# First stage of a fused attention and linear block laid out anew, and an order rule for the tiled matmuls

## The reference, cut to what matters

```python
def _layernorm(x): return (x - mean(x)) / sqrt(var(x) + 1e-5)

# x: (4, 2048, 512) float32; Wq, Wk, Wv, Wp: (512, 512); 16 heads of 32
h = _layernorm(x)
q, k, v = heads(h @ Wq + bq), heads(h @ Wk + bk), heads(h @ Wv + bv)
att = q @ k.T / sqrt(32)
att = where(tril and (column % 4 != 3), att, -inf)     # every fourth key is never seen
y = softmax(att) @ v
x = x + _layernorm(y @ Wp + bp)
# one of eight (512, 512) matrices is chosen by argmax(log_softmax(logits) - log(-log(u)))
x = x + _layernorm(_layernorm(x) @ W[idx] + b[idx])
```

## Time and profile before

| | us |
|---|---|
| median of 3 runs | 2775.3 |
| lowest, highest of them | 2772.9, 2775.33 |
| the profiled execution | 2770.63 |
| its span, first to last instruction | 2768.8 |
| TensorE busy | 2555.6 (92%) |
| VectorE busy | 1972.0 (71%) |
| ScalarE busy | 1615.7 (58%) |
| GpSimd busy | 1484.0 (54%) |

### The profile page before, as it was taken

The page is one execution under the profiler, slowest core; times in us unless marked ns, Lnnn a source line. Parts: engine busy times, 40 slices in busy tenths (PEclk is TensorE's granted clock), DMA queues, the critical chain, the costliest instruction groups (busy, mean ns, idle before and its releaser), DMA issues.

```text
span 2768.8 us, 46168 instructions
## 1 busy us (share of the span) xinstructions
PE 2555.6 (92%) x17416; PEld 1014.9 (37%) x17416; DVE 1972.0 (71%) x4199; ACT 1615.7 (58%) x2781; POOL 1484.0 (54%) x1350
## 2 busy tenths in 40 slices
PE   1999999999999999999999999999999999999985
PEld 0444333333343433333344433333334343333222
DVE  8667876876587687787566778678647767677623
ACT  4556656666655566566665555666665565655662
POOL 2335465665546366376653547467455635546563
PEclk7999999999999999999999999999999999999997
DMA  4211110010021111001011211101002110100000
GB/s 130 76 33 55 36 46 21 22 41 16 25 64 54 39 37 48 15 26 40 11 50 48 63 37 45 33 14 41 11 21 68 50 33 25 51 16 18 20 1 19
DMA packets 89192, 103.98 MB, mean 38 GB/s; under 512 B 11562, under 2 KB 61578, under 8 KB 88970
## 3 DMA queue, kind: packets, MB, share of 16 engines
q1 hardware_dynamic: 88970, 101.04, 12.3%
HBM read 39.59 MB, written 16.78 MB: 20 GB/s over the span
## 4 chain that ended last, share of the span: by engine, by line
PE 64%; DVE 22%; ACT 5%; POOL 4%; issue 3%; DMA 1%; SPq 1%; POOLq 0%; ACTq 0%; DVEq 0%
PE psO L1045 13%; PE psM L1004 11%; PE psS L1028 10%; DVE MP L807 9%; PE psU L1061 8%; PE psW L981 7%; PE psW L982 6%; PE psW L983 6%; ACT P L710 3%; DVE SC L826 2%; DVE STA L773 2%; DVE XR L785 2%; PE psS L1031 1%; DVE XP L793 1%; PE psM L1007 1%
## 5 line engine op out<-in xcount | busy, mean ns | idle before, releaser
L710 ACT ACTIVATE P<-psS,EX 128x512 f32<-128x512 f32 (+2 forms) x1920 | 1122.0, 631 | 668.3 <-PE psS L1028 357.4
L807 DVE TENSOR_REDUCE MP<-psM 128x1 f32<-128x512 f32 (+8 forms) x2112 | 1107.8, 560 | 502.1 <-PE psM L1004 269.0
L581 POOL TENSOR_TENSOR P<-P 128x512 f32<-128x512 f32 x576 | 725.5, 1288 | 119.6 <-ACT P L710 118.9
L1004 PE MATMUL psM<-KST,QST 96*128 96x512 f16 (+8 forms) x2112 | 640.0, 335 | 59.1 <-DVE MP L807 47.2
L1028 PE MATMUL psS<-QST,KST 98*128 98x512 f16 (+2 forms) x1920 | 618.9, 357 | 29.5 <-ACT P L710 22.3
L1045 PE MATMUL psO<-P,V 128*32 128x512 f32 (+2 forms) x3840 | 463.2, 554 | 10.6 <-ACT P L710 8.9
L586 POOL TENSOR_TENSOR SC<-SC 128x512 f32<-128x512 f32 x64 | 83.7, 1307 | 554.9 <-DVE SC L826 554.9
L1004 PEld LDWEIGHTS psM<-KST,QST 96*128 96x128 f16 x2112 | 200.8, 97 | 466.6 <-DVE MP L807 272.4
L1028 PEld LDWEIGHTS psS<-QST,KST 98*128 98x128 f16 x1920 | 171.1, 97 | 405.2 <-issue 190.0
L1061 PE MATMUL psU<-P,ONES 128*32 128x512 f32 (+2 forms) x2688 | 299.3, 517 | 0.0
L826 DVE RECIPROCAL SC<-SC 128x128 f32<-128x128 f32 x256 | 231.7, 929 | 79.5 <-ACT SC L718 79.5
(11 more groups left out here) (129 smaller groups left out, 3152.7 us busy)
## 6 DMA issues: line engine op xcount, KB each, us to landing
XB<-in_L_attn_x_dram SPq DMA_DIRECT2D x64, 256.0 KB, 2.7
XR<-in_L_attn_x_dram SPq DMA_DIRECT2D x64, 256.0 KB, 2.7
QST<-QKH SPq DMA_DIRECT2D x128, 128.0 KB, 3.2
out_dram<-XR SPq DMA_DIRECT2D x64, 256.0 KB, 2.0
KST<-QKH SPq DMA_DIRECT2D x128, 96.0 KB, 2.6
QST<-QKL SPq DMA_DIRECT2D x64, 128.0 KB, 3.3
KST<-QKL SPq DMA_DIRECT2D x64, 96.0 KB, 2.7
QST<-MROW SPq DMA_DIRECT2D x128, 4.0 KB
```

What stands on the lines that cost most here:

```text
L581: e.tensor_tensor(P[:, acc, a, :], P[:, acc, a, :], P[:, buf, a, :], ALU.add).then_inc(g_s, 1)
L710: e.activation(P[:, p_buf[u, g, sb_], a, t0:512], psS[:, s_slot[step] % 2, t0:512], ACT.Exp, scale=EX[:, 1:2]).then_inc(a_e, 1)
L807: e.tensor_reduce(MP[:, j, r, a, ci:ci + 1], psM[:, m_slot[s] % 2, 0:n], AX.X, ALU.max).then_inc(v_m, 1)
L1004: i = e.matmul(psM[:, k, 0:n], QST[0:96, h, 128 * r:128 * r + 128], KST[0:96, h, c0:c0 + n], start=True, stop=not last)
```

## The change

1. Loads on two queues. SyncE issues x, the two small rows, the identity, then the biases; ScalarE issues Wk, Wq, Wv, the mask and Wp (`load_w` is now a step of ScalarE). `choose` is cut in two on VectorE, and constants are written first.
2. Wider splits. `whigh` and `wlow` of Wq and Wk are 4 instructions of 128x512 each in place of 16 of 128x128.
3. `absmax` is cut into one step for each matrix (`wmax`), one for the biases (`bmax`) and the all-reduce (`allmax`, 1200 ns in the table). Wp, the chosen matrix and the fold get late ranks (0.1 to 0.5); the fold is cut in three, and projections wait for the split of their own weight alone. A pseudo engine `hbm` stands for the landing of the weights in the scheduler.
4. In the scheduler, when TensorE's last step was a `pv` or a `sum`, a ready `pv` or `sum` is taken before any other step.

```diff
-        add("sp", -99, 9000, ("load_w",), [("sp", "load_x", 0, 3)])
-        add("act", -99, 5500, ("choose",), [("sp", "load_w")])
-            add("gp", (-90, -65)[n], 3000, ("absmax", n), [("dve", "absmax", n)])
+        add("act", -100, 2600, ("load_w",))
+        for i, n in enumerate((1, 0, 2, 3)):
+            add("hbm", -100 + i, 2700, ("land", n), [("act", "load_w")])
+        for n, at in enumerate((-89, -90, -88, 0.1, 0.15)):
+            add("dve", at, 2250, ("wmax", n), [("hbm", "land", n), ("dve", "consts")])
+        for n, at in enumerate((-87, 0.2)):
+            add("gp", at, 1200, ("allmax", n), [("dve", "bmax"), ("dve", "scales", 0)][n:n + 1]
+                + [("dve", "wmax", i) for i in ((0, 1, 2), (3, 4))[n]])
...
+        for n, at in ((1, -60), (0, -59), (2, -58), (3, 0.3), (4, 0.4)):
+            add("act", at, 2400 if n < 2 else 2000, ("whigh", n), [("dve", "scales", int(n > 2))])
+            add("dve", at, 2400, ("wlow", n), [("act", "whigh", n)])
...
+        add("dve", 0.5, 3200, ("fold", 2), [("dve", "fold", 1), ("dve", "wlow", 3), ("dve", "wlow", 4)])
...
-                for at, (rank, key) in enumerate(ready[e]):
+                tiled = e == "pe" and self.pe and self.pe[-1][0] in ("pv", "sum")
+                for at, (rank, key) in sorted(enumerate(ready[e]),
+                                              key=lambda x: tiled and x[1][1][1] not in ("pv", "sum")):
...
+                if kind == "load_w":
+                    for n, w in ((1, Wk), (0, Wq), (2, Wv)):
+                        e.dma_start(stage[n], w.rearrange("(k p) n -> p k n", p=128)).then_inc(d_w[n], 16)
...
-                        for k in range(4):
-                            for m in range(4):
-                                c = slice(128 * m, 128 * m + 128)
-                                e.activation(WH[:, n, k, c].rearrange("p (d a) -> p a d", a=4),
-                                             stage[n][:, k, c].rearrange("p (a d) -> p a d", a=4), ACT.Copy,
-                                             scale=SW[:, n:n + 1]).then_inc(a_w, 1)
+                        for a in range(4):
+                            e.activation(heads_apart(WH, n, a), heads_in(stage[n], a), ACT.Copy,
+                                         scale=SW[:, n:n + 1]).then_inc(a_w, 1)
```

More of the change, by code:

```diff
@@ L68, in __init__ @@
             self.finish(u)
-        self.pe, self.act, self.dve, self.gp, self.sp = ([] for _ in range(5))
+        self.pe, self.act, self.dve, self.gp, self.sp, self.hbm = ([] for _ in range(6))
         self.run()
@@ L87, in startup @@
-        add("act", -98, 5400, ("kconst",), [("dve", "consts")])
[L88 to L93, removed]
@@ L178, in attend @@
                     was = self.P_WAS.get((u, g, sb))
-                    held = [("dve", "wlow", 2)]
+                    held = [("dve", "wlow", n) for n in range(3)]
                     if was:
@@ L423, in sandwich_block @@
         DV = counted(order.dve, lambda s: {
-            "choose": ("p", 6), "consts": ("c", 8), "absmax": ("p", 2 if s[-1] else 6),
-            "scales": ("p", 7 if s[-1] else 19), "wlow": ("w", 16 if s[-1] in (0, 1) else 1),
-            "fold": ("f", 18 if s[-1] else 1), "stats": ("ln", 4), "norm": ("n", 1), "cast": ("n", 1),
+            "choose": ("p", 4 if s[-1] else 2), "consts": ("c", 7), "ident": ("c", 1), "wmax": ("p", 1), "bmax": ("p", 3),
+            "scales": ("p", 7 if s[-1] else 19), "wlow": ("w", 4 if s[-1] in (0, 1) else 1),
+            "fold": ("f", 17 if s[-1] == 2 else 1), "stats": ("ln", 4), "norm": ("n", 1), "cast": ("n", 1),
             "high": ("q", 1), "peak": ("m", 1), "peaks": ("m", 3), "invert": ("o", 1)}[s[0]])
         GP = counted(order.gp, lambda s: {
-            "absmax": ("c", 1), "rstd": ("ln", 1), "low": ("p", 1), "rest": ("q", 1), "add": ("s", 1),
+            "allmax": ("c", 1), "rstd": ("ln", 1), "low": ("p", 1), "rest": ("q", 1), "add": ("s", 1),
             "scale": ("o", 1), "olow": ("o", 1), "add_x": ("r", 1), "add_y": ("r", 1)}[s[0]])
+        staged = max(DV["wlow", n] for n in range(3))
         w_job = [s[1] if s[0] == "proj" else s for s in order.pe
@@ L672, in _ @@
                     elif name == "v":
-                        ac.wait_ge(v_w, WV)
                         if u:
@@ L901, in _ @@
                                   ).then_inc(v_f, 1)
-                elif kind == "fold":
+                elif kind == "fold" and s[1] == 1:
                     dv.wait_ge(p_w, PE["fold",])
```

141 lines of the change are left out of this document (78 added, 63 removed).

## The result

The change made the kernel a little slower: 2776.8 us (12 runs, 2773.3 to 2782.6) beside 2773.6 for the kernel before in the same comparison, a ratio of 1.0018 with a 95% interval of 1.0010 to 1.0026 (the quotient of the two medians alone is 1.0012). That is within the 0.2% named above, and 12.9 us over the 2763.9 that was forecast, outside the range. Two single executions, one of the kernel before at 5625.6 us and one of a later experiment at 3708.3 us, lie far off all others and count in no ratio. The profiled execution has a span of 2774.9 us (before 2768.8).

What follows compares the result with a forecast made beforehand. TensorE was taken to bound the body, after a first stage of some 83 us where it hardly works. Gains of 10 (body) and 1.4 (first stage) made 11.4 us, so 2763.9 us from a median of 2775.3; range 2752 to 2774.

Steps and rivals of the forecast that it cites:

- The body: Attention after the first stage, TensorE-bound: 49 fewer groups of tiled matmuls save 11.8 us, of which 10 us reach the end.
- how much reaches the end: Body: 85% of TensorE's 11.8 us saving shortens the run, the rest lost to new waits; 10 us.
- The price of a group: Body: each switch between whole-array and tiled matmuls saved is worth 0.24 us of TensorE's time; 49 saved.
- a clock of 0.50 behind idle time: First stage: TensorE's granted clock at 60 to 70 us, so its first microseconds cost double, about 1.3 us lost.
- TensorE's busy time down by about 12: Sign expected in the new profile's body: single groups replaced by pairs, TensorE busy about 12 us less.
- Idle time behind 100 us grows by more than 5: Sign that would prove the forecast wrong: TensorE's idle time after 100 us growing by more than 5 us.
- The first stage: Work before the first peak, some 83 us: VectorE reads that peak at 82 instead of 83.5, 1.4 us earlier.
- the splits of Wk and Wq: First stage, VectorE: four wide instructions take 2.8 us per weight, so 5.6 in place of 9.5.
- A: Rival, body: waits for VectorE's maxima leave at best half the groups' gain; 2771 us; chance 0.17 shared with D.
- C: Rival, body: pairs held together starve ScalarE, TensorE waits for exponentials; 2794 us, or 2782 with 0.4 a regrouping; chance 0.07.
- B: Rival, first stage: second GpSimd code change overlapped or short, first peak at 68 or 72; 2754 us; chance 0.14.
- D: Rival, body: cost lies in changing psO to psU, so merged groups save nothing; 2771 us; chance 0.17 shared with A.

Runs made afterwards that it cites:

- rule alone: Kernel before plus only the scheduler's preference for a ready `pv` or `sum` after a `pv` or `sum`: 2772.2 us, ratio 0.9988 to before.
- outside the short units: Kernel before plus the scheduler's `pv`/`sum` preference, except while a block is in its first key tile (units with j = 0): 2760.0 us, ratio 0.9936.
- stage alone: Changed kernel with the scheduler's `pv`/`sum` preference taken back: 2776.2 us, ratio 1.0006 to the kernel before.

## Why the prediction was wrong

**The body, 10 us forecast, 3 measured.** The step that failed is "how much reaches the end": 85%, argued from new waits and their length only. It had no term for the granted clock in the body. With the rule alone the waits it allowed for came, 3.7 us more idle, twice the 1.8 of its 15%. But they came in lumps of 1 to 2 us, and behind such lumps the clock fell: 6.7 us' worth by the runs, 9.0 by the traces. The price of a group stands on the whole: the rule's work at full clock is 14.2 us less where 11.8 were forecast, right outside the short units and too low in them. The prediction even had the row that would have warned it, a clock of 0.50 behind idle time, and used it for the first stage alone.

**What the new profile would show.** "TensorE's busy time down by about 12" failed: up 6.6. "Idle time behind 100 us grows by more than 5" would have called the forecast wrong; it didn't (from the first score on 156.6 against 152.7), and the forecast was wrong nevertheless: idle time was the wrong gauge. The busy time together with the granted clock is the right one.

**The first stage, 1.4 forecast, about nothing measured.** All-reduce at 25 (25.35), work behind it at 33.6 (33.12), scales at 36 (35.44), splits at 42 (41.35), the second all-reduce's end and way back at 65.4 (67.58), right to some 2 us. The changes of code that the profile shows took 7.38, 6.31 and 6.78, where 7.6, 6.0 and 7.3 were used. The step that failed is the splits of Wk and Wq, 5.6 forecast and 9.36 measured, 3.8 us: its upper bound came from a statistics instruction that reads whole rows, and the row of the same operation with the same spacing, 0.30 for 128 elements, would have given 4 x 0.30 = 1.2 each. As the instructions overlap a little, 3.5 of it reach the chain. The fold took 0.6 more (75.03 to 84.34), the change ahead of the second all-reduce 0.3. Won back were 0.65 (the splits began earlier), 0.4 (GpSimd's rest ended 1.3 behind the split of Wv, not 1.7), 0.5 (the change behind the second all-reduce took 6.78, not 7.3) and 0.7 (the last split and `high` took 2.5, not 3.2), so that the peak came 2.2 late. The prediction also stopped at the first peak and took for granted that the rest moves with it, but the first score came 4.1 later than before.

**Rivals.** A comes closest in time, with 2773.9 where nothing is given back (its 2771 stands for a quarter of the groups' 11.8, where its text says half, which would be 2768), but not in kind: the body does give back. C's mild case of 2782 is as near on paper, for another reason. B's point, that code changes hold the chain, was right as a lever, about 15 us, though not as a forecast: the change itself kept all four. C's scores did not starve: waits for exponentials went from 22.3 to 19.2. D is out: the merged groups save 14.2 us of TensorE's work.

**What doesn't add up.** Rule alone at 0.9988 and stage alone at 1.0006 would together give 0.9994, and the change has 1.0018. Its runs have a mean clock of 0.9804 where the rule's 0.9781 and the stage's shorter time at the low level would let one expect 0.982; at 1.8 us for 0.001 that is some 3 of the 7 us. The traces say where the rest may lie. The first score starts at 98.6 and 100.5 before, at 99.8 with the rule alone, at 105.1 with the stage alone and at 102.7 and 105.6 in the changed kernel; from there to the end it is 2671.5 with the rule alone and 2672.3 and 2666.7 in the changed one. So behind the first score the change is no worse than the rule alone, and what it loses against it stands ahead of it. Why more time at the low level comes when the two meet stays open.

## What to carry to other kernels

Where TensorE is the bound, price a reordering in two currencies: the time of the instructions it saves, and the granted clock, which here fell where waits of one to two microseconds were bunched, and took back most of what many short savings earned. Counting busy time at the low level half shows the two apart. Look for the few places where a new order bunches such waits, and try to exempt them; here that turned 3 us into 17, of which some 8 are shorter waits that nobody had foreseen. In a serial first stage, count changes of GpSimd's code and spaced accesses before the width of instructions or the number of queues.

## What the runs showed of the hardware

- Within one kernel, run-to-run differences of some 8 us (medians of 2768.9 to 2777.3) go with the granted clock: 1.8 us for each 0.001 of its mean, over 68 runs between 0.980 and 0.984.
- TensorE's work at full clock, its busy time with the part at the low level halved, came back to 0.5 us in two executions of one kernel whose spans differ by 9.0.
- A write of fp16 at every fourth element costs nearly twice on ScalarE (1.18 against 0.63 for 128x512); on VectorE it is 1.17 against 0.67, with one fp16 input spaced as well. Reading fp32 at every 32nd element costs at least as much, 0.37 for 128x128 on VectorE.
- An all-reduce takes GpSimd 0.39 (1.15 once), and a change of code that goes with it 6.0 to 7.6. In its place, two small fp32 products and two VectorE operations were done 3.5 us after the last maximum (24.6 to 28.1).
